# Attention block kernel: steps of three score units, values one step behind, a second piece per step

## The reference

```python
x = x + attn(layernorm(x))                    # causal attention
x = x + ffn(layernorm(x))
# attn: Q, K, V = x @ W.T in 16 heads; softmax(Q K.T / 4, causal) V; @ o_proj.T
# ffn:  base = x @ W.T + b; logits = x @ gate_w.T + gate_b
#       top 2 of 8 experts, gates = softmax of the two logits
#       out = base + sum over the two of gate * (x @ lora_A[e].T) @ lora_B[e].T
```

## Time and profile before

| what | value |
|---|---|
| median of three runs | 393.42 us |
| the profiled execution's own time | 393.18 us |
| its span, first to last instruction | 391.4 us |
| mean granted TensorE clock | 0.975 of 2.4 GHz |
| TensorE busy, matmuls | 354.2 us in 2558 instructions |
| ScalarE busy | 279.5 us in 317 |
| VectorE busy | 209.7 us in 711 |
| GpSimd busy | 47.8 us in 75 |
| first step of chunk 1 | at about 64 us |
| first steps of chunks 2 and 3 | at about 131 and 232 us |
| last values, then the tail | at 365.3 us |

### The profile page before, as it was taken

The page is one execution under the profiler, slowest core; times in us unless marked ns, Lnnn a source line. Parts: engine busy times, 40 slices in busy tenths (PEclk is TensorE's granted clock), DMA queues, the critical chain, the costliest instruction groups (busy, mean ns, idle before and its releaser), DMA issues.

```text
span 391.4 us, 6977 instructions
## 1 busy us (share of the span) xinstructions
PE 354.2 (90%) x2558; PEld 138.0 (35%) x2558; DVE 209.7 (54%) x711; ACT 279.5 (71%) x317; POOL 47.8 (12%) x75
## 2 busy tenths in 40 slices
PE   8967978899998999999999999998999899799874
PEld 3545524354333444423323233232322323222542
DVE  4555558455755654555447464546346543600785
ACT  2544438677887877888788887888878688799311
POOL 5011000000011100011121111211112111100040
PEclk9997969999999999999999999999999999999997
DMA  6479444222450022271000000000000000000001
GB/s 202 139 224 315 116 131 141 55 55 54 124 148 13 2 54 75 62 214 44 13 2 13 3 13 16 3 13 2 13 16 0 16 0 15 13 2 3 0 3 55
DMA packets 29380, 23.31 MB, mean 60 GB/s; under 512 B 15392, under 2 KB 25888, under 8 KB 29344
## 3 DMA queue, kind: packets, MB, share of 16 engines
q1 hardware_dynamic: 29344, 22.84, 19.8%
HBM read 12.35 MB, written 10.49 MB: 58 GB/s over the span
## 4 chain that ended last, share of the span: by engine, by line
PE 63%; DVE 20%; ACT 7%; issue 6%; POOL 2%; DMA 1%; DVEq 0%; ACTq 0%
PE acc L713 23%; PE scores L696 12%; PE aux L596 7%; ACT probs L814 6%; PE aux L651 5%; PE aux L637 3%; DVE probs L1010 2%; PE aux L662 2%; PE aux L602 2%; PE aux L623 1%; DVE ffn L1055 1%; POOL exp_gap L1216 1%; PE aux L644 1%; DVE gates L1083 1%; DVE parts L954 1%
## 5 line engine op out<-in xcount | busy, mean ns | idle before, releaser
L814 ACT ACTIVATE probs<-scores 128x1024 f32<-128x1024 f32 x272 | 260.2, 1032 | 69.1 <-PE scores L696 59.1
L713 PE MATMUL acc<-probs,v_aug 128*32 128x512 f32 (+3 forms) x1280 | 145.4, 545 | 1.3 <-ACT probs L814 0.9
L696 PE MATMUL scores<-q_stack,k_stack 64*128 64x512 f16 (+3 forms) x640 | 86.5, 352 | 3.7 <-ACT probs L814 2.0
L696 PEld LDWEIGHTS scores<-q_stack,k_stack 64*128 64x128 f16 x640 | 21.1, 94 | 103.6 <-ACT probs L814 80.3
L1010 DVE TENSOR_TENSOR probs<-probs,mask_sb 128x512 f32<-128x512 f32 (+1 forms) x80 | 44.2, 577 | 22.5 <-ACT probs L814 22.0
L713 PEld LDWEIGHTS acc<-probs,v_aug 128*32 128x32 f32 x1280 | 30.8, 110 | 49.8 <-issue 29.7
L596 PE MATMUL aux<-xT,wqkv_sb 128*128 128x128 f32 x192 | 26.3, 294 | 1.0 <-DVE xT L941 1.0
L596 PEld LDWEIGHTS aux<-xT,wqkv_sb 128*128 128x128 f32 x192 | 24.0, 203 | 5.4 <-issue 3.1
L952 DVE CAST parts<-qk 128x512 f16<-128x512 f32 x12 | 5.1, 427 | 36.5 <-ACT qk L806 36.5
L1207 POOL TENSOR_TENSOR rstd<-ve,minus_half 128x1 f32<-128x1 f32 x12 | 7.3, 608 | 101.6 <-DVE ve L932 101.6
L1211 POOL TENSOR_TENSOR rstd<-ve,minus_half 128x1 f32<-128x1 f32 x12 | 6.6, 549 | 103.8 <-DVE ve L1040 103.8
(11 more groups left out here) (146 smaller groups left out, 323.0 us busy)
## 6 DMA issues: line engine op xcount, KB each, us to landing
q_stack<-q_dram SPq DMA_DIRECT2D x32, 128.0 KB, 2.8
k_stack<-k_dram SPq DMA_DIRECT2D x32, 128.0 KB, 2.8
qk_dram<-qk SPq DMA_DIRECT2D x12, 256.0 KB, 2.5
x_sb<-x SPq DMA_DIRECT2D x3, 512.0 KB, 6.4
q_dram<-parts SPq DMA_DIRECT2D x12, 128.0 KB, 2.0
k_dram<-parts SPq DMA_DIRECT2D x48, 32.0 KB, 1.9
out<-result SPq DMA_DIRECT2D x12, 128.0 KB, 1.7
qk_dram<-probs SPq DMA_DIRECT2D x4, 256.0 KB, 3.3
```

The costliest lines, as they stand in the source:

```text
L696: m = pe.matmul(scores[u % BANKS][:, j, col:col + n], k_stack[row:row + STACK, kb // TPC, 2 * i + p, kb % TPC * P:(kb % TPC + 1) * P], q_s ...
L713: m = pe.matmul(acc[32 * hp:32 * hp + 32, lo:CHUNK], v_aug[:, kb, QUAD * i + hp, :], probs[:, u % PROBS, hp % 2, col:col + CHUNK - lo], st ...
L814: act.activation(probs[:, u % PROBS], scores[u % BANKS][:], ACT.Exp, scale=EXP_SCALE).then_inc(exp_done, 1)
```

## The change

Behind chunk 0 a step has three units instead of two; the tables `STEP_OF` and `UNITS_OF` say which. Chunks 1 to 3 then have 84 steps of scores instead of 126. A group stands one step behind its last unit (in chunk 0 still two). The first group of a quad has no step more; it only may not share a step with the last group of the quad before. `place_pieces` may put a second piece behind the values in chunks 1 to 3, where the first one isn't `project_qk` and the work placed so far is behind an even share (`WORK`, `rate`). VectorE's step takes the masks ahead of `LATER`; and behind chunk 0 it masks a step's first two units already at the end of that step and the third at the start of the next. ScalarE's copy of `project_qk` stands behind the third unit.

```diff
--- before.py
+++ after.py
@@ -83,7 +83,10 @@
 
 UNITS, GROUPS = lay_out_attention()
 FIRST_UNIT = [min(u for u, x in enumerate(UNITS) if x.c == c) for c in range(NCHUNK)] + [len(UNITS)]
-FIRST_STEP = [u // 2 for u in FIRST_UNIT]
+
+STEP_OF = [u // 2 if u < FIRST_UNIT[1] else FIRST_UNIT[1] // 2 + (u - FIRST_UNIT[1]) // 3 for u in range(len(UNITS))]
+FIRST_STEP = [STEP_OF[u] for u in FIRST_UNIT[:NCHUNK]] + [STEP_OF[-1] + 1]
+UNITS_OF = [[u for u in range(len(UNITS)) if STEP_OF[u] == s] for s in range(FIRST_STEP[NCHUNK])]
 QK_STEPS = FIRST_STEP[NCHUNK]
 
 
@@ -95,7 +98,10 @@
     at = {}
     s = 0
     for n, g in enumerate(GROUPS):
-        s = max(s, (last_unit(g) + 4) // 2 + (1 if g.first else 0))
+        u = last_unit(g)
+        s = max(s, STEP_OF[u] + (2 if u < FIRST_UNIT[1] else 1))
+        if g.first and n - 1 in at.get(s, ()):
+            s += 1
         at.setdefault(s, []).append(n)
     return at
 
@@ -121,11 +127,20 @@
 POST_GAP = {"turn_sums": 1, "turn_back": 1, "o": 2, "turn_y": 1, "ffn": 2, "turn_gated": 1, "lora": 1}
 
 
+
+WORK = {"turn_x": 256, "project_qk": 1024, "project_v": 512, "norm_q": 256, "norm_k": 256, "turn_sums": 512,
+        "turn_back": 256, "o": 512, "turn_y": 256, "ffn": 784, "turn_gated": 128, "lora": 256}
+
+
 def place_pieces():
 
     at = {}
     post_next = 0
     flying = []
+
+    done = 0
+    rate = (sum(WORK[name] for name in POST_PIECES) * (TILES - TPC) + sum(WORK[name] for name in PRE_PIECES) * 2 * TPC
+            ) / (QK_STEPS - FIRST_STEP[1] - 8)
     for c in range(NCHUNK):
         pre = []
         if c + 1 < NCHUNK:
@@ -136,18 +151,23 @@
                 pre += [("norm_q", 0), ("norm_k", 0)]
             pre += [("norm_q", c + 1), ("norm_k", c + 1)]
         for s in range(FIRST_STEP[c], FIRST_STEP[c + 1]):
-            for slot in range(2 if c == 0 else 1):
-                if pre:
+            for slot in range(2):
+                if pre and (c == 0 or slot == 0):
                     at[s, slot] = pre.pop(0)
+                    done += WORK[at[s, slot][0]] if c else 0
+                    continue
+                if c == 0:
                     continue
                 if len(flying) < 2 and post_next < TILES - TPC and s > SUMS_STEP[post_next // TPC]:
                     flying.append([post_next, 0, s])
                     post_next += 1
                 ready = [f for f in flying if f[2] <= s]
-                if ready and slot == 0:
+                if ready and (slot == 0 or (s, 0) in at and at[s, 0][0] != "project_qk"
+                              and done < rate * (s + 1 - FIRST_STEP[1])):
                     f = ready[0]
                     name = POST_PIECES[f[1]]
                     at[s, slot] = (name, f[0])
+                    done += WORK[name]
                     f[1] += 1
                     f[2] = s + POST_GAP[name]
                     if f[1] == len(POST_PIECES):
@@ -716,9 +736,8 @@
                 m.then_inc(pv_done, 1)
 
             def step(s):
-                for u in (2 * s, 2 * s + 1):
-                    if u < len(UNITS):
-                        scores_of(u)
+                for u in UNITS_OF[s] if s < QK_STEPS else ():
+                    scores_of(u)
                 piece(s, 0)
                 for n in GROUPS_AT.get(s, ()):
                     values_of(n)
@@ -813,9 +832,9 @@
                     act.wait_ge(pv_done, USED_BY[u - PROBS])
                 act.activation(probs[:, u % PROBS], scores[u % BANKS][:], ACT.Exp, scale=EXP_SCALE
                                ).then_inc(exp_done, 1)
-                if u % 2 == 1:
+                if u == UNITS_OF[STEP_OF[u]][-1]:
                     for slot in range(2):
-                        name, n = PIECE_AT.get((u // 2, slot), (None, None))
+                        name, n = PIECE_AT.get((STEP_OF[u], slot), (None, None))
                         if name == "project_qk":
                             store_qk(n)
 
@@ -1121,12 +1140,14 @@
                     POST[name](n, buffers(n))
 
             def step(s):
-                before = PIECE_AT.get((s - 1, 0), (None, None))
-                if before[0] in LATER:
-                    after_piece(LATER[before[0]], before[1])
-                for u in (2 * s - 2, 2 * s - 1):
-                    if 0 <= u < len(UNITS) and UNITS[u].masked:
+
+                for u in UNITS_OF[s - 1][0 if s <= FIRST_STEP[1] else 2:] if 1 <= s <= QK_STEPS else ():
+                    if UNITS[u].masked:
                         clear_later_keys(u)
+                for slot in range(2):
+                    before = PIECE_AT.get((s - 1, slot), (None, None))
+                    if before[0] in LATER:
+                        after_piece(LATER[before[0]], before[1])
                 if (s, 0) in PIECE_AT:
                     name, n = PIECE_AT[s, 0]
                     after_piece(name, n)
@@ -1136,6 +1157,9 @@
                 if (s, 1) in PIECE_AT:
                     name, n = PIECE_AT[s, 1]
                     after_piece(name, n)
+                for u in UNITS_OF[s][:2] if FIRST_STEP[1] <= s < QK_STEPS else ():
+                    if UNITS[u].masked:
+                        clear_later_keys(u)
 
             def general():
                 dve.wait_ge(gen_band_in, 16)
```

## The result

The changed kernel takes **398.33 us** (median of 20 runs, 393.74 to 401.52), the kernel before on the same chip 393.75 (20 runs, 391.81 to 395.75). The ratio is **1.0092, 95% interval 1.0065 to 1.0119**: slower, by about 3.6 us (0.92%), where 2 us less had been forecast. Two of its 20 runs were slow ones (401.52 and 400.7), and the ratio is taken over the other runs, so it says less than the 4.6 us between the medians. 398.33 lies above the end of the forecast range, 397. The profiled run took 398.09 us.

The account below looks back on a forecast made before the run. TensorE was taken to bound chunks 1 to 3 and ScalarE the last 14 steps. The terms -8.7 + 7.3 + 1.4 - 2.0 sum to -2.0 us: 391.2 for the profiled run, 391.4 as a median, range 386 to 397.

Parts of the forecast that it names:

- fewer starts: TensorE in chunks 1 to 3: 42 fewer score starts and 30 fewer value runs, -8.7 us.
- ScalarE's pace: Chunks 1 to 3: less even steps make TensorE wait for exponentials, 13.7 us instead of 6.4, +7.3.
- VectorE's waits against the 13.1 before: Behind chunk 0: TensorE's old 13.1 us of waits go, new ones of 14.5 come, +1.4.
- clock behind chunk 0: Chunks 1 to 3: the sum has no term for stretches at the lower clock, so 0.
- unplaced, carried at 2.5: TensorE in the old chunks 1 to 3: 2.5 us not placed, left as they are.
- chunk 0: Each quad's first group comes one step earlier, partly filling TensorE's wait for VectorE: -2.0 us, at most about 2.5.
- Rival 3: TensorE: bursts cost nothing to start, so the saving from fewer starts falls away, 399.9 us; chance 0.04.
- the piece and the first group cover: VectorE's masks: beyond waits of 1.5 us in steps 15, 18, 35, 55 and 0.2 at 25, none make TensorE wait.
- The copies of steps 50 and 86: Behind steps 49 and 85: gates and normalising ahead of VectorE's acc copy cost 1.7 us each beyond the pace wait.
- The gated ranks: turn_gated after an ffn that is a second piece: TensorE waits 1.2 us four times, 4.7 in all.
- The second: VectorE's single queue becomes the bound, acc copies waiting at all twelve quad ends: +5.5, 397 us; chance 0.2.
- Rival 1: Waits for VectorE and pace overlap by 5 us, and a low-clock stretch saves another 1: 385.5 us; chance 0.21.

Follow-up runs that it names:

- experiment 5: Changed kernel with VectorE copying finished sums ahead of project_qk's splitting, and masking a step's first two units ahead of sums copy and second piece: 391.04 us, ratio 0.9924.
- experiment 3: Changed kernel, but in steps with project_qk VectorE copies the finished sums ahead of the splitting: 392.58 us, ratio 0.9973.
- experiment 9: Changed kernel with steps of two units instead of three behind chunk 0, values still one step behind: 397.66 us, ratio 1.0096 to the kernel before.
- experiment 10: Changed kernel with steps of two units and values two steps behind again, leaving VectorE's mask order and chunk 0's part: 388.98 us, ratio 0.9881.
- experiment 4: Changed kernel with masks of a step's first two units ahead of the sums copy and second piece's handler on VectorE: 394.21 us, ratio 0.9995.
- experiment 8: Kernel before with only chunk 0's part: first groups of its first three quads one step earlier: 392.24 us, ratio 0.9964.
- experiment 1: Changed kernel with each mask cut to one column, so later keys are not cleared and the output differs: 391.36 us, ratio 0.9937.
- (6): experiment 5's kernel with gates behind turn_sums' or turn_x's handler after ffn, and turn_back swapping slots with turn_gated where they share a step: 387.75 us, ratio 0.9854.
- (12): Kernel of (6) with second pieces only where both total at most 1050 columns, even share reached 20 steps before the end: 386.33 us, ratio 0.9804.
- experiment 11: Changed kernel, steps of three kept, with each group of values two steps behind its last unit again: 428.18 us, ratio 1.0892.

## Why the prediction was wrong

The sum for the profiled run was -2.0 us; the two spans differ by +4.9. By the prediction's steps:

| step | predicted | measured | from |
|---|---|---|---|
| fewer starts and ScalarE's pace | -8.7, +7.3 | agree as a pair | 49 of 83 steps within 0.1 |
| VectorE's waits against the 13.1 before | +1.4 | +2.6 | 22.4 beyond the sum, without 3.7 in small pieces and 3.0 of the clock |
| clock behind chunk 0 | 0 | +3.0 | two low stretches, 1.5 each |
| start of chunk 0's scores | 0 | +1.5 | 23.18 against 21.68, 1.4 of it the clock's |
| unplaced, carried at 2.5 | 0 | +1.2 | those 3.7 |
| end of the last values | 0 | +0.5 | not placed |
| chunk 0 | -2.0 | -2.5 | from its first scores 39.9 against 42.4 |

**The step that failed is the clock's, which the sum puts at nothing.** I read the clock's lower level as a matter of chunk 0. In the kernel after it falls in steps 50 and 86 too, behind the light steps 49 and 85, and ahead of chunk 0. One stretch behind chunk 0 costs 1.5 us (experiment 5) to 1.6 (experiment 3), and the early one 1.4: the first projections (TensorE from 7.84 to 14.05 us) take 6.2 us, and 4.8 in the kernel before (7.55 to 12.37). That makes some 4.4 of the 6.9 us between -2.0 and +4.9 in the profiled execution. The same steps 85 and 86 run at the full clock in experiment 3's profile, with the same waits, so the waits alone don't bring the stretch. For the other runs there is only their mean clock (last section). The lengths from chunk 1's first scores to the last values, in four profiles:

| kernel | low stretches in it | length, us |
|---|---|---|
| before | 0 | 301.2 |
| after | 2 | 307.1 |
| experiment 9: two units, values one behind | 0 | 305.4 |
| experiment 10: two units, values two behind | 0 | 300.0 |

With its two stretches at 1.5 the kernel after would be at 304.1 (an estimate): 2.9 us above the kernel before, where the prediction had 0.0 (-8.7 + 7.3 + 1.4), and 1.3 below experiment 9.

**The starts and the pace held.** (42 x 0.11 + 30 x 0.14 is 8.8, not 8.7.) The bursts have gaps, as read from the earlier trace rows; a step of scores of three, `lora`, two groups and `ffn` took 4.75 us against 4.73 summed. Had bursts cost nothing to start, each step would have been 0.25 us shorter (0.11 + 0.14). The rule of the Trainium skill, "TensorE: Matmul & The Clock Gate", Part 2, that one tile's drain overlaps the next one's fill, is not what this trace shows between scores and values; what makes the gap is not shown. Rival 3 fell with it; that its 399.9 lies near 398.33 is luck. That the two terms nearly cancel, experiment 9 shows: steps of two and of three are within 0.7 us of each other.

**The VectorE term was too small by 1.2 us, and its waits stand elsewhere than I said.** The sentence that failed says that beyond steps 15, 18, 35, 55 and 25 "the piece and the first group cover" the masks. Steps 49 and 85 have no piece, so nothing covers them, and I hadn't asked what VectorE holds when they begin: a second piece of the step before, with residual and statistics. Masks came to 5.4 us by step times instead of 1.7. But at steps 49 and 85 this is mostly no addition. The copies of steps 50 and 86, summed at 1.7 each, are worth nothing there beyond the pace wait once the clock is taken out (0.99 and 1.35, less 1.5 each), since the mask's wait comes first; and experiment 4 shows that without it TensorE waits for exponentials, 0.4 us less for steps 85 and 86 together. What did add: step 55 cost 1.45 where I gave at most 0.9, and the copy behind step 12 2.45, not 0.9, since VectorE reached it only behind the five operations of the splitting, as in step 29. The gated ranks (4.9 against 4.7) and step 27 (1.69 against 1.5) were right.

**Chunk 0** gave 2.5 us from its own first scores on, the right size. It shows as 1.0 since those scores started 1.5 us late. The first scores of chunk 1 waited 1.0 us for keys, the limit that the prediction named. Part of the 2.5 is the clock's: the kernel before has 13.7 us at the lower level in its chunk 0, the kernel after none. Alone the edit is worth 1.4 by the ratio (experiment 8).

**The rivals.** The second, VectorE's single queue, named the right resource for the waits, the sign and almost the size (397); its mechanism, a copy at all twelve ends of quads, didn't hold: five waits of that kind are there. With 4.4 us of the clock's in the profiled execution, the near hit is luck in part. Rival 1 fell as a whole, but at steps 49 and 85 the two kinds of wait do overlap, as it says. Had the corners been asked for one by one, the answer was near: the change is three changes. By the ratios, order and chunk 0 alone give -4.7 us, values one step behind +8.5 (measured with steps of two), steps of three with second pieces -0.2; each of these carries the clock of its runs.

## What to carry to other kernels

When a group of work is moved one step nearer to what feeds it, each thing that an in-order engine does between the two loses a step of cover at once; go through the lightest steps first, since they have nothing to hide it with, and ask what that engine still holds from the step before. A wait that is taken away may only uncover another that stood behind it (experiment 4), so look at the step after it too. A wider step saves starts only if the buffers allow the old distance: here eight buffers forced the shorter one, and that cost more (8.5 us with steps of two) than wider steps gave (nothing measurable). Before accepting a new order as slow, try the cheap permutations of the in-order engine: three of them, and one swap of two pieces, turned 1.0092 into 0.9854. And before a difference of 1% between two profiles is put down to an order, compare where their low stretches of the clock stand.

## What the runs showed of the hardware

The time hangs on where the clock's low stretches fall, more than on how many there are: over their runs the two kernels have the same mean granted clock (0.979 after, 0.978 before). Each run lists its own:

| kernel | runs at the higher clocks | runs at the lower |
|---|---|---|
| before | 393.1 us (nine at 0.987) | 394.7 (eleven at 0.971) |
| after | 394.1 us (three at 0.988 to 0.991) | 399.35 (two at 0.971 and 0.973) |

A like difference of clock costs the old kernel 1.6 us and the new one 5.2. The profile of the one shows its low stretches in chunk 0 and the tail; that of the other shows one ahead of chunk 0, two in chunks 2 and 3, where TensorE is the bound, and one in the tail. The tail takes 26.1 us in both. That the other runs are of the same kind is argued from these two profiles, not shown. At the highest clocks seen the two kernels are 1.0 us apart (three runs and nine), so a good part of the measured 3.6 us seems to be clock; that is argued too. Low stretches between chunk 1's first scores and the last values stood also at 64.6 and 74.9 us (experiment 1), 205.5 (3), 74.0 (4), 335.9 (5), 206.2 (6), 302.0 (8) and 119.3 (12). So the eight profiles of kernels with steps of three have nine of them (only experiment 11 has none), the six with steps of two have one. Why one falls in a given run and place and not in another stays open: the steps 85 and 86 are the same in the change and in experiment 3, and one has it and the other hasn't.
